# Expert stage of an audio tower: slots written out, gathers issued ahead of stores, two PSUM banks for the down products

## The reference, cut to what matters

```python
h = _L0_tok_ref(x, ...)
h = h + _L0_attn_ref(_layernorm(h), ...)
h = h + _L0_ffn_ref(_layernorm(h), ...)

def _L0_ffn_ref(...):                       # E, T, C, H = 8 experts, 4080 tokens, 256, 512
    gates = softmax(x @ w_red @ wg_n.T)
    scores, idx = max(gates, axis=1), argmax(gates, axis=1)
    h = gelu(x @ W1[idx] + b1[idx])         # 256 -> 512, the chosen expert's
    o = h @ W2[idx] + b2[idx]               # 512 -> 256
    return o * scores
```

## Time and profile before

| | us |
|---|---|
| median of 3 runs | 576.51 |
| lowest and highest run | 574.85, 576.92 |
| the profiled execution | 576.19 |
| its span, first to last instruction | 574.4 |

### The profile page before, as it was taken

One profiled execution on the slowest core, in us unless ns is written; L12 is line 12 of the kernel. 1 busy time (PEld: TensorE's weight loads), 2 busy tenths in 40 slices (PEclk: granted clock), 3 DMA queues, 4 the chain that ended last, 5 costly groups with the idle time before them and its releaser, 6 DMA issues. The chain is left out here.

```text
span 574.4 us, 12975 instructions
## 1 busy us (share of the span) xinstructions
PE 516.6 (90%) x3425; PEld 366.1 (64%) x3426; DVE 460.2 (80%) x1220; ACT 231.1 (40%) x447; POOL 197.0 (34%) x285
## 2 busy tenths in 40 slices
PE   2989999999999999999889889998688898998982
PEld 1876667777666777666645677774365575665651
DVE  2668888898888898888988989999577887777771
ACT  1335545465545455654445312221043344443440
POOL 7452232322132223123211112221425655655532
PEclk9999999999999999999989979999799999999997
DMA  9311211221221220221130334435312222222210
GB/s 249 111 37 38 75 48 62 73 62 48 73 73 37 73 73 37 73 73 37 38 98 29 85 87 117 113 88 201 105 30 70 71 65 70 73 59 68 61 44 0
DMA packets 34985, 41.99 MB, mean 73 GB/s; under 512 B 8514, under 2 KB 26163, under 8 KB 34704
## 3 DMA queue, kind: packets, MB, share of 16 engines
q1 hardware_dynamic: 24908, 27.06, 15.7%
q0 software_dynamic: 3744, 9.34, 5.7%
q10 hardware_dynamic: 6308, 5.28, 3.2%
HBM read 32.97 MB, written 9.59 MB: 74 GB/s over the span
## 5 line engine op out<-in xcount | busy, mean ns | idle before, releaser
L521 PE MATMUL banks<-proj,xnT_h 128*128 128x512 f16 x384 | 114.5, 380 | 1.5 <-DVE early L1226 1.5
L502 PE MATMUL banks<-early 128*128 128x256 f16 x768 | 86.8, 273 | 2.5 <-DVE wo_l L1055 2.5
L502 PEld LDWEIGHTS banks<-early 128*128 128x128 f16 x768 | 75.1, 98 | 11.1 <-DVE wo_l L1055 2.7
L521 PE MATMUL banks<-proj,xnT_l 128*128 128x512 f16 x192 | 72.8, 379 | 0.0
L521 PEld LDWEIGHTS banks<-proj,xnT_h 128*128 128x128 f16 x384 | 37.6, 98 | 37.6 <-DVE early L1226 2.0
L1865 POOL DMA_INDIRECT out<-proj,vo x39 | 39.8, 1021 | 63.0 <-DVE vo L1688 38.1
L750 PE MATMUL banks<-w2h,vo 128*128 x312 | 57.7, 273 | 3.6 <-DVE proj L1686 2.6
L731 PE MATMUL banks<-w1h,vo 128*128 x156 | 53.8, 386 | 7.4 <-issue 4.7
L1859 POOL DMA_INDIRECT vo<-token_rows,vo x39 | 43.1, 1105 | 27.8 <-issue 27.8
L1002 ACT ACTIVATE vo<-banks 128x256 f16<-128x256 f32 x39 | 14.9, 383 | 89.7 <-PE banks L718 65.2
L1797 POOL TENSOR_TENSOR w1l<-stage,w1h 128x512 f32 (+1 forms) x16 | 18.9, 1183 | 83.7 <-ACT w1h L885 83.7
(11 more groups left out here) (261 smaller groups left out, 1261.4 us busy)
## 6 DMA issues: line engine op xcount, KB each, us to landing
early<-in_x SPq DMA_DIRECT2D x16, 512.0 KB, 3.4
stage<-in_W SPq DMA_DIRECT2D x32, 256.0 KB, 2.8
early<-lam_by_chunk SPq DMA_DIRECT2D x32, 68.0 KB
token_rows<-rows ACTq DMA_DIRECT2D x16, 129.0 KB, 2.4
early<-lam_by_head SPq DMA_DIRECT2D x16, 128.0 KB, 3.1
rows<-in_b SPq DMA_DIRECT2D x1, 2048.0 KB, 7.4
token_rows<-rows ACTq DMA_DIRECT2D x16, 112.9 KB, 2.1
vo<-in_tok_W ACTq DMA_DIRECT2D x2, 512.0 KB, 7.3
```

Of the source, the lines that this page charges most:

```text
L502: last = mm(bank(2 + j, D), x_[:, k, at:at + P], w[:, KG * half + k, :], start=(half == 0 and k == 0 and x_ is gT_h and w is wtok_h), stop ...
L521: last = mm(dst, a, c, start=(i == 0), stop=(i == n - 1))
```

## The change

1. On PE, ACT, DVE and POOL the 39 slots are written out; no loop is left in the expert stage, and every slot number is a constant. PE loads each expert once and keeps it in a register until its `down`.
2. POOL waits for `y_steps` of slot i (signalled by `finish` itself), issues the gather of slot i + 6 first and the store of slot i second. Before, the store came first, after `y_done`.
3. Ids are taken straight from the tables `gather_id` and `store_id`; the copy after `finish`, `ring_ids`, and two small operations ahead of the first slot go.
4. `down(i)` writes bank 3 or 6 by turns and waits for `finish(i - 2)` in place of `finish(i - 1)`.
5. DVE runs `norm_rows(i + 2)` after `split_gelu(i - 1)`, just ahead of `finish(i - 2)`; before, it stood ahead of `scaled_bias(i)`.
6. ACT runs `split_gelu(i - 1)` ahead of `gelu(i)`.

The diff, cut to its core:

```diff
             def down(i, w, e):
                 pe.wait_ge(s["g_done"], i + 1)
-                if not (isinstance(i, int) and i == 0):
-                    pe.wait_ge(s["y_steps"], i)
+                if i >= 2:
+                    pe.wait_ge(s["y_steps"], i - 1)
...
-                        last = mm(bank(3, D), a[:, w, f, :], w_[:, bass.ds(e * FC + f, 1), :].rearrange("p a b -> p (a b)"),
+                        last = mm(bank(3 + 3 * w, D), a[:, w, f, :], w_[:, bass.ds(e * FC + f, 1), :].rearrange("p a b -> p (a b)"),
...
-            slots(0, first=True)
-            with pe.Fori(1, ROUNDS) as g:
-                slots(g)
-            experts = slots(ROUNDS, REST, last=True)
...
+            experts = {0: expert_of(0)}
+            for i in range(SLOTS):
+                up(i, experts[i])
+                if i + 1 < SLOTS:
+                    experts[i + 1] = expert_of(i + 1)
+                    transpose_rows(i + 1)
+                if i >= 1:
+                    transpose_gelu(i - 1, (i - 1) % 2)
+                if i >= 2:
+                    down(i - 2, i % 2, experts[i - 2])
...
-                copy(ring_ids[:, w, :], slot_ids[:, bass.ds(i, 1), :].rearrange("p a v -> p (a v)")).then_inc(s["y_done"], 1)
...
-            with pool.Fori(0, ROUNDS - 1) as g_:
-                for w in range(RING):
-                    store(RING * g_ + w, w)
-                    load(w, ring_ids[:, w, 1:2])
...
+            pool.wait_ge(s["slot_ids_ready"], 1)
+            for i in range(SLOTS):
+                pool.wait_ge(s["y_steps"], i + 1)
+                if i + RING < SLOTS:
+                    load(i + RING)
+                store(i)
```

More of the change, by code:

```diff
@@ L751, in down @@
                                   start=(f == 0 and w_ is w2h and a is gh), stop=(f == FC - 1 and a is gl))
                 last.then_inc(s["m2_ready"], 1)
[L754 to L771, removed]
@@ L784, in _ @@
+            transpose_gelu(SLOTS - 1, (SLOTS - 1) % 2)
+            for i in (SLOTS - 2, SLOTS - 1):
+                down(i, i % 2, experts[i])
         @block.scalar
@@ L1011, in split_gelu @@
                 act.wait_ge(s["gt_ready"], i + 1)
-                if not (isinstance(i, int) and i < 2):
+                if i >= 2:
                     act.wait_ge(s["m2_ready"], i - 1)
                 af(gh[:, w].rearrange("p f t -> p (f t)"), bank(4 + w), ACT.Copy).then_inc(s["gh_done"], 1)
[L1016 to L1023, removed]
-            split_rows(0)
[L1026 to L1030, removed]
+            split_rows(0)
+            for i in range(SLOTS):
+                if i + 1 < SLOTS:
+                    split_rows(i + 1)
+                if i >= 1:
+                    split_gelu(i - 1, (i - 1) % 2)
+                gelu(i, i % 2)
+            split_gelu(SLOTS - 1, (SLOTS - 1) % 2)
         @block.vector
@@ L1687, in finish @@
                     ALU.add).then_inc(s["y_steps"], 1)
-                copy(ring_ids[:, w, :], slot_ids[:, bass.ds(i, 1), :].rearrange("p a v -> p (a v)")).then_inc(s["y_done"], 1)
-            def slots(g, count=RING, first=False, last=False):
-                for w in range(count):
-                    i = RING * g + w
-                    e = expert_of(i)
-                    add_bias(i, w % 2, e)
-                    if not (last and w == count - 1):
-                        split_rows(i + 1)
-                    if not (last and w >= count - 2):
-                        norm_rows(i + 2, (w + 2) % RING, g if w + 2 < RING else g + 1)
-                    scaled_bias(i, w, e)
-                    if not (first and w == 0):
-                        split_gelu(i - 1, (w - 1) % 2)
-                    if not (first and w < 2):
-                        finish(i - 2, (w - 2) % RING, g - 1 if w < 2 else g)
@@ L1706, in _ @@
             dve.wait_ge(s["experts_ready"], 1)
-            norm_rows(0, 0, 0)
+            norm_rows(0)
             split_rows(0)
-            norm_rows(1, 1, 0)
+            norm_rows(1)
             dve.wait_ge(s["biases_in"], 32)
-            slots(0, first=True)
-            with dve.Fori(1, ROUNDS) as g:
-                slots(g)
-            slots(ROUNDS, REST, last=True)
-            split_gelu(SLOTS - 1, (REST - 1) % 2)
-            finish(SLOTS - 2, REST - 2, ROUNDS)
-            finish(SLOTS - 1, REST - 1, ROUNDS)
+            for i in range(SLOTS):
+                e = expert_of(i)
+                add_bias(i, i % 2, e)
+                if i + 1 < SLOTS:
+                    split_rows(i + 1)
+                scaled_bias(i, i % RING, e)
+                if i >= 1:
+                    split_gelu(i - 1, (i - 1) % 2)
+                if i + 2 < SLOTS:
+                    norm_rows(i + 2)
+                if i >= 2:
+                    finish(i - 2)
@@ L1720, in _ @@
+            split_gelu(SLOTS - 1, (SLOTS - 1) % 2)
+            finish(SLOTS - 2)
+            finish(SLOTS - 1)
         @block.gpsimd
```

60 lines of the change are left out of this document (25 added, 35 removed).

## The result

The changed kernel takes 557.12 us, median of 4 runs (556.43 to 557.98); the kernel before, run beside it, 575.68 (574.15 to 576.92). The ratio is 0.968, with a 95% interval of 0.9657 to 0.9703. The forecast was 557.5 in a range of 555.5 to 563.5. The profiled execution took 557.67 us with a span of 555.9 at a mean granted clock of 0.98: 18.52 us less than the profiled one of before, where the sum of the prediction had said 18.75.

A forecast was written before the change was run, and what follows sets the result against it. PE was taken to bound the kernel at 3.26 us per slot; 16.95 us of stalls plus 1.8 in the tail, 18.75 us, came off 576.19, giving 557.5 us with the distance to the median, range 555.5 to 563.5.

The forecast's parts named there:

- What bounds the kernel: Expert stage: PE sets a floor of 3.26 us per slot; 16.95 us over 35 slots are stalls.
- Slots written out: PE at pass starts: loads placed after `up` get hidden, gap per slot zero; other bound 10.6 us.
- Gathers ahead of stores: POOL and DVE: gather 1.33 us earlier, 1.5 us of slack; 13.0 us of waits go, only partly on the path.
- What POOL then holds: POOL per slot: 2.55 us plus a gap of 0.30 to 0.87, so 2.85 to 3.42; low end taken.
- The rival in which POOL paces the kernel: POOL needs 1.07 us more after each DMA before the next behind a wait, 3.62 a slot: 563.5 us, chance 0.08.
- Normalisation later: DVE: normalisation moved behind `scaled_bias` and `split_gelu` costs nothing, with thin cover of 0.6 us less the hand-over.
- ACT's swap: ACT: gelu's high part reaches DVE about 0.6 us earlier, gelu as much later; also helps the tail's split.
- Two banks: `down` on PE: nothing more in steady slots beyond 2.6 us already counted; the tail gains 1.8 us.
- Code fetch: PE: about 7 more code packets; counted as hidden, rival has them stop PE, 574 to 608.5 us, chance 0.04.
- The other rivals: DVE's normalisation late (567.5 us, 0.05); loop-start stall stays (571.5, 0.03); code fetch not hidden on PE (608.5, 0.04).
- The sum: Whole kernel: 16.95 + 1.8 = 18.75 us off 576.19 gives 557.4; with the distance to the median, rounded, 557.5.

The follow-up runs named there:

- experiment 2: Changed kernel, all written out, with PE's 12 extra register loads at the loop's places but no loop or branch: 558.04 us, ratio 0.9716.
- experiment 1: Changed kernel with PE's slots back in the hardware loop, other engines still written out: 566.02 us, ratio 0.9843.
- experiment 6: Kernel before with PE's slots written out and the gather ahead of the store on POOL, all else as before: 564.22 us, ratio 0.9824.
- experiment 3: Changed kernel with the store ahead of the gather again on POOL: 558.27 us, ratio 0.9708.
- experiment 10: Changed kernel with only the normalisation early on DVE, ahead of the scaled bias, gathers still first: 562.58 us, ratio 0.9767.
- experiment 11: Changed kernel with ACT's old order, gelu(i) ahead of split_gelu(i - 1): 560.04 us, ratio 0.9727.
- experiment 7: Changed kernel with bank 3 alone for the down products, so down(i) waits for finish(i - 1): 557.65 us, ratio 0.9693.
- experiment 4: Kernel before with only PE's slots written out: 571.51 us, ratio 0.9946.
- experiment 5: Kernel before with only the gather of slot i + 6 put ahead of the store of slot i on POOL: 572.21 us, ratio 0.995.
- experiment 8: Changed kernel with the normalisation early on DVE and the store ahead of the gather on POOL: 568.47 us, ratio 0.989.
- experiment 12: Changed kernel with 22 filler products on PE ahead of the expert stage in place of 14: 556.51 us, ratio 0.9671.

## Why the prediction was right, point by point

*What bounds the kernel.* Right. PE's pace of 3.26 us per slot, read from slots 3 to 5, holds for all 35 slots, and the stalls counted against it were those that went: 16.96 of 16.95.

*Slots written out.* The size was right, the reason half wrong. The loads beside the branch were held for the cause; by themselves they are 1 to 2 us (experiment 2), and it takes the loop, at 8.9 with them (experiment 1), to lay them open. Also wrong was the silent assumption that the stalls at the passes are PE's own. PE's loop on the best surroundings costs 8.9 us, PE's loop with one bank 11.8. The rest of the passes' stalls is not traced to one cause: experiment 6, with ACT, DVE and POOL in loops and PE not, keeps 0.45 a pass, and no run has one of these three loops alone.

*Gathers ahead of stores.* Right: 0.80 us from `finish` to the gather where 0.90 was used, POOL's instructions 1.02 each where the gather had 1.23, and no wait for a gather. The slack is larger than the 1.5 us of the prediction: the normalisation starts 4.94 us after the gather, for 3.04 in the earlier trace rows, which leaves 1.9. But experiment 3 shows that this edit is worth only 1 to 2 us beside the others.

*What POOL then holds.* A gap of 0.93 before each gather, above the 0.87 given as the upper bound and far above the low end taken, though below the 1.07 of the earlier trace rows. It is a wait for `finish`, so nothing hangs on it; when POOL is behind, the gap is 0.31 (experiment 10 has such gathers). The rival in which POOL paces the kernel had the gap as a cost that is paid always, and it isn't. The long gathers, 1.23 us in the earlier trace rows, are gone too: no DMA of POOL in the expert stage is over 1.04 now. Before, 13 gathers took more than 1.12, and 12 of them ended 0.30 us after the end of DVE's split of gelu beside them, so DVE seems to hold up POOL as well.

*Normalisation later.* "It costs nothing" was right, and "this cover is thin" too. What failed is the step that counted the move as only harmless: it is worth 5.5 us (experiment 10), by way of gathers in time, of PE's late signals, and perhaps of an instruction out of POOL's way. The contention could be seen before: the line of the normalisation in the earlier trace rows has one of 0.581 us, and 8 at 0.48 and above. The prediction wrote that nothing but one long gather showed a contention. The Trainium skill, "SBUF — State Buffer", section "Who interferes with whom", says that a `tensor_scalar` can take the port pair that DVE shares with GpSimd, and that the second to come then blocks. The trace agrees in that the end is fixed by POOL and not by the start. It adds that of the 1.02 us of POOL's DMA only the last part does so, since normalisations that ended within its first 0.86 us kept to 0.40 or 0.41; and one that was already running for up to 0.4 us was held as well.

*ACT's swap.* Counted at nothing in the steady slots; undone it costs 2.9 us (experiment 11).

*Two banks.* Right: nothing in the steady slots, the tail's 1.80 measured where 1.8 was predicted. But the prediction gave all of it to the bank, and the bank itself is 1.0 us (experiment 7); the other 0.8 goes with the other moves, and no run says which.

*Code fetch.* Right: 7 more packets on PE's queue and 5 more on the second, all hidden. The prediction's other thought, that the stalls at the passes could be fetches after a taken branch, is not borne out: in experiment 1 four of them pass without a packet for PE. *The other rivals* did not occur: no slot above 3.27 after slot 3, no "issue" gap on PE.

*The sum.* Its last step is off: 557.44 with the 0.32 to the median gives 557.8, not 557.5. The rest came out since it went by the pace with nothing late and not by adding what each edit gives. Added, the single edits would have misled: 3 us and 3 us give 11 (experiments 4 to 6), and 1 us and 5.5 us taken away give 11.3 (experiments 3, 8 and 10). That it met the gain in the 35 slots to 0.01 us is luck: the stalls were read from one execution, and those of the kernel before scatter by 2.8 us.

## What to carry to other kernels

When two limits lie over each other, take the floor from a stretch in which neither acts, and ask of a set of edits whether it removes all that stands above that floor; the gain of one of them alone says little about the set. Look at the spread of a short instruction's duration as well as at its median: 403 to 581 ns in one line was a contention, and at another place in the same queue it was gone (what it cost by itself is not shown). Before you call a register load or a branch cheap, see how far the sequencer is ahead of its engine: the same two loads were hidden with the lead and open without it. And try a later place for the consumer of a late transfer as well as an earlier one for its producer: taking back the first cost 5.5 us here, the second 1 to 2.

## What the runs showed of the hardware

An indirect DMA instruction takes POOL 1.02 us, and another queued behind it starts 0.31 later; from a `finish` on DVE to the start of the gather that waits for it are 0.80. Toward its end it holds up a 128x256 f32 normalisation on DVE, which then ends 1.09 to 1.14 us after the DMA's start; `finish` on DVE, which reads PSUM, kept its 0.47 to 0.49 us beside it.

A loop of PE with five branches of at most 0.209 us costs 8.9 us, although over the whole kernel it fetches less code (12 packets in experiment 1's queue q8, 19 in the changed kernel's). The branches' own durations and the loads by themselves (1 to 2 us) don't add up to it; PE's sequencer loses its lead at the branch, and two loads that were hidden then leave 0.83 us of idle time.

In experiments 6, 8 and 10 some of PE's signals are recorded 1.4 to 2.3 us after the end given for the last product, and in the changed kernel none between 424 and 545 us over 0.6. The cause is open.

The first `up` of the expert stage took 4.2 us to the second in the profiles of some kernels (before, changed, experiments 1, 6, 8, 10) and 2.8 in the others, by the clock granted after the idle time ahead of it. That is 1.4 us, more than separates the medians of experiments 2, 3, 7 and 12 from the changed kernel's (0.5 to 1.2 us).
